# A three-stage decoder layer on one core: the start-up reordered, the mask analysed earlier, and the output transposes taken apart

## The reference, cut to what matters

```
x = x + self_attention(layernorm(x))       # 16 heads of 16; down (256 -> 16*64) and up (64 -> 16)
                                           # weights; half of each head is rotated (cos, sin)
x = x + cross_attention(layernorm(x), ctx, mask)      # mask (512, 512), True = key may be seen
x = x + mixture(layernorm(x))                         # router, top 512 tokens of 8 experts, two matmuls
```

## Time and profile before

| | |
|---|---|
| median of three runs | 1333.94 us (1333.66 to 1336.55) |
| the profiled execution: its own time | 1336.71 us |
| the profiled execution: first to last instruction | 1335.0 us |
| mean granted TensorE clock | 0.924 of full |
| first `st` matmul | 86.29 us |
| busy share PE / DVE / ACT / POOL | 86% / 76% / 51% / 39% |

### The profile page before, as it was taken

One profiled execution on the slowest core, in us unless ns is written; L12 is line 12 of the kernel. 1 busy time (PEld: TensorE's weight loads), 2 busy tenths in 40 slices (PEclk: granted clock), 3 DMA queues, 4 the chain that ended last, 5 costly groups with the idle time before them and its releaser, 6 DMA issues. The chain is left out here.

```text
span 1335.0 us, 22038 instructions
## 1 busy us (share of the span) xinstructions
PE 1144.6 (86%) x7591; PEld 681.5 (51%) x7592; DVE 1017.3 (76%) x2733; ACT 680.2 (51%) x1359; POOL 518.5 (39%) x712
## 2 busy tenths in 40 slices
PE   4389999999999999999999999999995115999994
PEld 2255546455455554445454454544343004988984
DVE  4778778888888778889888898988852884766651
ACT  4015455554545555666656566666661103556551
POOL 6365563754748332324232323231021003445432
PEclk9569899998999999999999999999997556999997
DMA  5431523515345253342525252423111502545422
GB/s 172 108 85 43 112 76 87 120 39 111 81 111 121 78 123 83 101 105 79 112 65 112 65 111 75 102 71 74 34 48 34 161 1 96 163 111 109 112 23 26
DMA packets 90416, 118.06 MB, mean 88 GB/s; under 512 B 13057, under 2 KB 60161, under 8 KB 90178
## 3 DMA queue, kind: packets, MB, share of 16 engines
q1 hardware_dynamic: 84162, 108.12, 31.6%
q0 software_dynamic: 6144, 8.52, 3.8%
HBM read 48.76 MB, written 16.91 MB: 49 GB/s over the span
## 5 line engine op out<-in xcount | busy, mean ns | idle before, releaser
L739 ACT ACTIVATE probs<-ps_st 128x512 f32<-128x512 f32 (+3 forms) x1024 | 477.5, 518 | 345.9 <-PE ps_st L583 340.9
L601 PE MATMUL ps_p<-kst,qst 63*128 63x512 f32 (+3 forms) x1024 | 381.9, 435 | 10.9 <-DVE mx L827 8.3
L583 PE MATMUL ps_st<-qst,kst 64*128 64x512 f32 (+3 forms) x1024 | 358.6, 419 | 16.3 <-ACT probs L739 14.7
L825 DVE TENSOR_REDUCE mx<-ps_p 128x1 f32<-128x512 f32 x512 | 323.1, 681 | 19.7 <-PE ps_p L601 18.6
L583 PEld LDWEIGHTS ps_st<-qst,kst 64*128 64x128 f32 x1024 | 165.7, 188 | 267.1 <-ACT probs L739 206.7
L827 DVE CUSTOM_DVE_ANT_0 ps_p<-ps_p,tri 128x128 f32<-128x128 f32 (+3 forms) x512 | 238.5, 514 | 18.6 <-PE ps_p L601 15.6
L564 PE MATMUL ps_o<-probs,vals 128*32 128x512 f32 (+3 forms) x2048 | 234.6, 531 | 13.8 <-POOL probs L475 13.8
L601 PEld LDWEIGHTS ps_p<-kst,qst 63*128 63x128 f32 x1024 | 170.6, 190 | 40.4 <-DVE mx L827 17.8
L422 POOL TENSOR_SCALAR lnw<-mv 128x4 f32<-128x4 f32 x24 | 5.6, 234 | 346.5 <-DVE mv L811 346.5
L475 POOL TENSOR_SCALAR_AFFINE_SELECT probs<-probs 128x512 f32<-128x512 f32 x128 | 79.1, 633 | 91.8 <-ACT probs L739 91.8
L1189 PE MATMUL moe_ps_y<-moe_w,moe_hid_h 128*128 128x256 f32 x512 | 94.7, 283 | 0.0
(11 more groups left out here) (203 smaller groups left out, 1879.5 us busy)
## 6 DMA issues: line engine op xcount, KB each, us to landing
qst<-qk_h SPq DMA_DIRECT2D x64, 256.0 KB, 4.8
kst<-qk_h SPq DMA_DIRECT2D x64, 256.0 KB, 5.0
qst<-qk_l SPq DMA_DIRECT2D x32, 256.0 KB, 5.5
kst<-qk_l SPq DMA_DIRECT2D x32, 256.0 KB, 5.2
moe_w1r<-in_w_dram SPq DMA_DIRECT2D x8, 1024.0 KB, 5.2
moe_w2r<-in_w_dram SPq DMA_DIRECT2D x8, 1024.0 KB, 8.9
xin<-in_x_dram SPq DMA_DIRECT2D x8, 512.0 KB, 4.0
xres<-in_x_dram SPq DMA_DIRECT2D x8, 512.0 KB, 3.9
```

Source lines behind the costliest of these rows:

```text
L583: last = nc.tensor.matmul(out, kst[rows, t % 2, pair, kt * P:(kt + 1) * P], qst[rows, t % 2, pair, lo:S], start=True, stop=not masked)
L601: last = nc.tensor.matmul(ps_p1[:, i % 3, 0:keys], qst[rows, t % 2, pair, qt * P:(qt + 1) * P], kst[rows, t % 2, pair, 0:keys], start=True ...
L739: nc.scalar.activation(probs[:, kt, j, 0:n], ps_st[:, i % 2, 0:n], ACT.Exp, scale=float(DH) ** -0.5).then_inc(exp_done, 1)
L825: nc.vector.tensor_reduce(mx[:, g % 2, at:at + 1], bank, AX.X, ALU.max).then_inc(max_done, 1)
```

## The change

Seven things are changed.

1. The mask is loaded ahead of the three `down` arrays, and VectorE analyses it right after `ln` 0. The counting matmuls go ahead of fold 0 and between turn 0 and fold 2. The 0/1 copy goes into a view of `xres` (`mask_ones`), so that the scaled copy can be made at once. Only the last piece (the key row) stays behind the four `qk` on TensorE and the rotations on VectorE.
2. ScalarE fills both `kst` (zeros) and `qst` (ones): buffer 0 at the start, by four activations, buffer 1 after the weights, by four more. GpSimd's memset of `qst` is gone. The row of ones is copied into `kst` for each buffer, just ahead of its first `stack`.
3. `xload` 1 is issued behind the rope table, ahead of `wc` and the small arrays; it waits for `xn` of batch 0.
4. `ln` 1 goes from behind the four `stack` and `qk` steps of turn 0 to in front of the first `qk`, for VectorE and GpSimd alike.
5. `xt` 1 and the first `qk` of turn 1 go together behind `v`, ahead of the first `p1`; the other three `qk` of turn 1 move 7 to 9 units ahead (old units of the four -29, -21, -13, -5, new -45, -28, -21, -14).
6. In every turn `ot` 0 goes from unit 19 to unit 3 of the turn after; it waits only for `og` of the second group.
7. The waits for the mask chain and for the row of ones move to where they are needed (`p1`, `st`).

```diff
     for t in range(TURNS):
         far, near, own, after = (SPAN * (t + i) for i in (-2, -1, 0, 1))
         put(far - SPAN + 14, "xload", t)
-        put(far + 10, "ln", t)
-        put(far + 23, "xt", t, 0)
-        put(far + 27, "xt", t, 1)
+        put(far + (-34 if t == 1 else 10), "ln", t)
+        put(far + (17 if t == 1 else 23), "xt", t, 0)
+        put(far + (18 if t == 1 else 27), "xt", t, 1)
         for i in range(4):
-            put(far + (35, 43, 51, 59)[i], "qk", t, i // 2, i % 2)
+            put(far + ((19, 36, 43, 50) if t == 1 else (35, 43, 51, 59))[i], "qk", t, i // 2, i % 2)
-        put(after + 19, "ot", t, 0)
+        put(after + 3, "ot", t, 0)
         put(after + 19, "ot", t, 1)
...
+            sp.dma_start(mask_u8, dram["mask_t"].rearrange("(a p) c -> p a c", p=P)).then_inc(mask_loaded, 16)
             for i in range(3):
                 sp.dma_start(down[i].rearrange("p (a c) -> p a c", a=8),
                              dram["down_t"][i].rearrange("(a p) c -> p a c", p=P)).then_inc(down_loaded[i], 16)
             sp.dma_start(late[:, :, :], dram["rope"].rearrange("a p s -> p a s")).then_inc(rope_loaded, 16)
-            sp.dma_start(mask_u8, dram["mask_t"].rearrange("(a p) c -> p a c", p=P)).then_inc(mask_loaded, 16)
+            xload(1)
...
-            nc.gpsimd.memset(qst[:, :, :, :].bitcast(F32), 1.0).then_inc(qst_ones, 1)
             nc.gpsimd.memset(vals[:, :, :, :].rearrange("p a b c -> p (a b c)"), 1.0).then_inc(pool_prep, 1)
+            run(STEPS[first:second])
             pool.wait_ge(rope_loaded, 16)
             pool.wait_ge(small_loaded, 80)
-            run(STEPS[first:])
+            run(STEPS[second:])
...
-                        pe.wait_ge(m_free, M[("og", GROUPS * t + 3)] + 1)
+                        pe.wait_ge(m_free, M[("og", GROUPS * t + 1 + 2 * k)] + 1)
...
+            pe.wait_ge(mask_chain, 1)
+            for kt in range(TT):
+                last = nc.tensor.matmul(ps_m[:, 0, :], ones, mask_ones[:, kt, :], start=(kt == 0), stop=(kt == TT - 1))
+            last.then_inc(mask_mm, 1)
             pe.wait_ge(up_loaded, 32)
             fold(0)
             fold(1)
             turn_weights(0)
+            pe.wait_ge(mask_chain, 5)
+            nc.tensor.matmul(ps_m[:, 1, 0:TT], ones, differs, start=True, stop=True).then_inc(mask_mm, 1)
             fold(2)
             turn_weights(1)
+            pe.wait_ge(mask_chain, 6)
             run(STEPS[:first], False)
             turn_weights(2)
             run(STEPS[first:second], False)
...
+            def clear(buf):
+                for rows, value, done in ((kst, zero, kst_zero), (qst, unit, qst_ones)):
+                    for half in range(2):
+                        nc.scalar.activation(rows[:, buf, 4 * half:4 * half + 4, :], value[:, :].unsqueeze(2).to_broadcast([P, 4, S]),
+                                             ACT.Copy).then_inc(done, 1)
-            act.wait_ge(zero_made, 1)
+            act.wait_ge(zero_made, 2)
             clear(0)
-            clear(1)
             raw(0)
-            clear(2)
             raw(1)
...
-            clear(3)
             act.wait_ge(wc_loaded, 16)
             nc.scalar.activation(wo[:, 0, :, :], wc_raw.rearrange("p (a c) -> p a c", a=KT), ACT.Copy).then_inc(prep_hi, 1)
+            clear(1)
```

More of the change, by code:

```diff
@@ L321, in _ @@
                 kind = s[0]
-                if kind == "xload" and s[1] > 0:
+                if kind == "xload" and s[1] > 1:
                     xload(s[1])
@@ L405, in _ @@
             nc.gpsimd.memset(zero[:, :], 0.0).then_inc(zero_made, 1)
+            nc.gpsimd.memset(unit[:, :], 1.0).then_inc(zero_made, 1)
             nc.gpsimd.memset(up[:, :, :], 0.0).then_inc(up_zero, 1)
@@ L684, in _ @@
             run(STEPS[first:second], False)
-            pe.wait_ge(mask_chain, 1)
+            pe.wait_ge(mask_chain, 8)
             for kt in range(TT):
[L687 to L691, removed]
-            for kt in range(TT):
-                last = nc.tensor.matmul(ps_st[:, 1, kt * P:(kt + 1) * P], key_cols[:, kt, :], identb[:, :], start=True, stop=True)
+                last = nc.tensor.matmul(ps_p1[:, 0, kt * P:(kt + 1) * P], key_cols[:, kt, :], identb[:, :], start=True, stop=True)
             last.then_inc(mask_mm, 1)
@@ L924, in _ @@
             second = STEPS.index(("xt", 0, 1)) + 1
-            third = STEPS.index(("ln", 1)) + 1
+            third = STEPS.index(("qk", 0, 1, 1)) + 1
             nc.vector.memset(ones, 1.0)
             run(STEPS[:first])
+            dve.wait_ge(mask_loaded, 16)
+            mask_link(nc.vector.tensor_scalar(out=mask_ones, in0=mask_u8, scalar1=1.0, scalar2=None, op0=ALU.mult))
+            mask_link(nc.vector.tensor_scalar(out=lower_t[:, :, :], in0=mask_u8, scalar1=BIG, scalar2=-BIG, op0=ALU.mult, op1=ALU.add))
+            dve.wait_ge(mask_mm, 1)
+            mask_link(nc.vector.tensor_scalar(out=some_key[:, :], in0=ps_m[:, 0, :], scalar1=1.0, scalar2=None, op0=ALU.min), False)
+            nc.vector.tensor_reduce(keepers, lower_t[:, :, :], AX.X, ALU.max)
+            mask_link(nc.vector.tensor_reduce(keep_all, lower_t[:, :, :], AX.X, ALU.min))
+            mask_link(nc.vector.tensor_tensor(out=differs, in0=keepers, in1=keep_all, op=ALU.subtract), False)
+            dve.wait_ge(mask_mm, 2)
+            mask_link(nc.vector.tensor_reduce(vary_sum, ps_m[:, 1, 0:TT], AX.X, ALU.add))
+            nc.vector.tensor_scalar(out=vary[0:1, 0:1], in0=vary_sum[0:1, 0:1], scalar1=0.0, scalar2=None, op0=ALU.is_gt)
+            mask_link(nc.vector.tensor_scalar(out=alike, in0=vary_sum, scalar1=0.0, scalar2=None, op0=ALU.is_equal))
+            mask_link(nc.vector.tensor_tensor(out=key_cols, in0=keepers.unsqueeze(2).to_broadcast([P, TT, P]),
+                                              in1=alike.unsqueeze(2).to_broadcast([P, TT, P]), op=ALU.mult), False)
             low_qk(0)
@@ L934, in _ @@
             run(STEPS[second:third])
-            dve.wait_ge(mask_loaded, 16)
-            mask_link(nc.vector.tensor_scalar(out=lower_t[:, :, :], in0=mask_u8, scalar1=1.0, scalar2=None, op0=ALU.mult))
             dve.wait_ge(prep_hi, 4)
```

36 lines of the change are left out of this document (13 added, 23 removed).

## The result

The changed kernel takes **1316.37 us** (median of 4 runs, 1314.4 to 1317.02) against 1333.8 for the kernel before in the same comparison (4 runs, 1332.57 to 1336.55): a ratio of 0.9862, 95% interval 0.9848 to 0.9876. It is 1.4% or 17.4 us faster. The profiled execution took 1315.83 us with a span of 1314.1. The span before was 1335.0, so between the profiled executions there are 20.9 us; of the 3.5 us by which this is more than the 17.4, 2.9 are the distance of the profiled execution of before from its median and 0.5 that of after.

A forecast was written before the change was run, and what follows sets the result against it. A chain across engines was taken to bound the start-up, and TensorE, nearly always busy, the turns. Start-up -5.5, `ot` 0 -1.7 and last turn -0.7 made -7.9 us: 1333.94 becomes 1326 us, range 1318 to 1332.

The forecast's parts named there:

- the term for `ot` 0: Seven self-attention turns: moving `ot` 0 saves 0.25 us each, -1.7 us in all, bounds -4 and +2.
- rival 1: Self-attention turns: TensorE's clock may not fall where `ot` 0 goes, at most -10 us; under 1322 us, chance 0.17.
- my signs of being wrong: Whole kernel: turns after the first grow, or the first `st` comes later than 84 or earlier than 77 us.
- Rival 3: First units of a turn: `ot` 0 delays the scores serially, about +15 us over fifteen turns, 1342 us; chance 0.04.
- Cross-attention: Cross-attention turns: TensorE is packed in both places of `ot` 0, so 0 us, bounds -2 and +2.
- The tail: Last turn: `y` waits for the chain of one half less, -0.7 us.
- The start-up: Up to the first `st`: it comes at 80.8 instead of 86.29 us, -5.5 us, bounds -3 and -9.
- `ln` 1 on GpSimd: Start-up, ahead of GpSimd's first rotation: normalizing batch 1 takes between 5.3 and 7.5 us, half way taken.
- From there to the first `st`: Start-up, behind the last `qk` of turn 1: `shift` sets 7.1 us instead of 1.92, giving back 5.2.
- Rival 2: Start-up: slower rotations and late stacks eat the gain, leaving 0 to -2 us, 1332 to 1334; chance 0.12.
- 5.7 us lost and 15.3 won around `ln` 1: Start-up: third rotation 5.7 us later; last rotation to first `qk` of turn 1 takes 9.3 us instead of 24.6.
- the stacks of turn 0: Start-up: they land by 53 to 54 us, about when the `qk` is through, losing at most 1 us.

The follow-up runs named there:

- experiment 1: Kernel before with only `ot` 0 moved, from unit 19 to unit 3, and its wait: 1321.37 us, ratio 0.9898.
- Experiment 2: Changed kernel with `ot` 0 put back to unit 19: 1331.01 us, ratio 0.9971.
- experiment 3: Kernel before with four useless transposes of `ident` added at unit 3 of turns 1 to 7: 1327.92 us, ratio 0.9949.
- experiment 4: Kernel before with eight useless transposes of `ident` added at unit 3 of turns 1 to 7: 1327.7 us, ratio 0.9954.
- Experiment 5: Kernel before with `ot` 0 at unit 10 instead of 19: 1343.57 us, ratio 1.0077.
- experiment 6: Kernel before with only the mask load and analysis moved early: 1328.77 us, ratio 0.9957.
- experiment 7: Changed kernel with `ln` 1, `xt` 1 and the four `qk` of turn 1 at their old units: 1315.09 us, ratio 0.9861.
- Kernel 10: Changed kernel with GpSimd's half of `ln` 1 behind both its turn 0 rotations, `xt` and `qk` of turn 1 at old units: 1311.3 us, again 1315.95.

## Why the prediction was wrong

**The step that failed is the term for `ot` 0.** I put -0.25 us a turn and -1.7 in all, with bounds of -4 and +2. Turns 1 to 7 gave 12.2 us, and experiment 1 alone 13.2. Two things were wrong in it. The direct part was halved: I let the copy of ScalarE weigh against the shorter stretch, but the first group did not grow (5.54 against 5.56), so the 0.6 us of the third group came nearly whole: -3.9 instead of -1.7. And the clock was left out of the term and given to rival 1 with a chance of 0.17, though its price was worked out from the right rows: "five turns of 2.0 give -10 at the utmost", and 1326 less 10 is the time that was measured, in part by luck: the clock gave about 8 us, and most of the rest is the direct part. What I held against the rival was that an earlier start-up redraws the stretches. Experiment 2 shows that their sum stays: 328.68 us in six turns after a shift of 6 us. My own row said where to look: the stretch lay across the first sixteen units of a turn, whose first eight are the lightest in the turn, TensorE busy 4.25 of 5.56 us. The Trainium skill, "TensorE: Matmul & The Clock Gate", section "What's actually happening", has activity lift the clock; experiments 3 and 4 agree with it (1327.92 and 1327.7 us with work added), and I had cited it beside the rival without letting it move the chance. None of my signs of being wrong showed this: the turns did not grow, and the first `st` lay between 77 and 84; none of them asked whether the stretches would go.

**Rival 3, `ot` 0 on the scores' path,** did not come at unit 3: the first group takes what it took. Experiment 5 shows that the danger was real seven units later, where the room is gone: +1.28 us in that group at clock 1.00, and slower in all.

**Cross-attention:** forecast 0, measured -1.1 us in seven turns, inside the bounds of -2 and +2, and `ot` 0's own: experiment 1 takes 427.2 us for them, experiment 2 428.2, as before. **The tail:** I had -0.7; the `y` of the last turn still waits 1.53 us for `ot_l` (before 1.69), and the rest of the program is 0.7 us longer. The term is 0.

**The start-up** was right as a mechanism and near in size. Between the two profiled executions the first `st` moved by -8.1 us (86.29 to 78.22), against -5.5 forecast and inside the bounds of -3 and -9. But the same start-up as before also runs in experiments 1, 3, 4 and 5, with the first `st` at 84.65, 85.32, 84.12 and 85.13, and that of the changed kernel in experiment 2 and in its repetition, at 79.8 and 78.66. The means are 85.1 of five and 78.9 of three: -6.2 us, and the 8.1 compares the latest of the one with the earliest of the other. Step by step, in the two profiled executions:

- Loads, forecast +0.7: the fold that started at 14.09 starts at 14.47, so +0.4, and the first `qk` of turn 0 is no later than before (22.34 against 22.84).
- The mask, forecast 0: right, and `ln` 0 beside it took GpSimd 6.5 us (8.27 to 14.8), hidden as worked out.
- `ln` 1 on GpSimd, forecast half way between 5.3 and 7.5 us: it took 6.7 (24.66 to 31.38). Longer instructions beside VectorE's rotation are in the row (2.77 us for the four, against 2.18 in the earlier trace rows, while VectorE ran its rotation until 29.91, three instructions of which have two inputs in SBUF), as the Trainium skill, "SBUF — State Buffer", section "Who interferes with whom", has it. The third rotation came at 36.16, forecast 37.8 (whose lower bound, 31.2 and 5.5, is 36.7 and not 36.5; nothing hangs on it).
- The first `qk` of turn 1 at VectorE: 52.07, forecast 54.5. The first `p1` near 54: 54.18.
- The spacing of the four: 19.65 us in all, forecast 19.2. The last at 71.72, forecast 73.7.
- From there to the first `st`: 6.5 us, forecast 7.1. TensorE did not wait for `shift`, as I had said that it would: `shift` was issued at 75.15, the second transfer 0.7 later, and the `st` that needs it runs 3.07 us after the first issue. So it landed in less than 2.4 us; I had 3.3, by a neighbour of another size. The view of TensorE's waits from 28 to 79 us has no `shift` in it:

```profile
PE ps_m L545 <- DVE rope L872: 8.4, 1, 8.4
PE ps_p L609 <- DVE mx L836: 6.9, 5, 4.2
PE ps_m L623 <- DVE vals L893: 2.9, 1, 2.9
PE ps_p L609 <- DMA kst<-qk_h: 2.2, 1, 2.2
PE ps_m L545 <- DVE xt_l L847: 1.6, 1, 1.6
```

Its columns are the wait, its time in all, how often and the longest.

Rival 2, the gain eaten in the rotations, did not come either, though `ln` 1 took nearly its price: the first `st` is 6 to 8 us earlier, not 0 to 2.

But I read the gain wrongly in one respect, which the sum hid: it needs none of the new units. The early mask gives all of it (experiment 6), and the step that I priced most closely, 5.7 us lost and 15.3 won around `ln` 1, is the mask alone: 12.5 of the 15.3 are its old place, and the new units, with the 5.7 that they cost, net to nothing (experiment 7). What is late next is not in my list of waits with its right weight: the stacks of turn 0. From 37.50 to the first `p1` all 16 DMA engines are busy throughout (share 1.03):

```profile
37.50:54.18 16.68, 10.04 (x38) 8.38 (x39) 11.29 (x19) 1.19 (x2) 5.21 (x4) 0.65 1.03 217
```

I had "about when the `qk` is through; at most 1 us is lost"; TensorE lost 2.15 there, and GpSimd, whose rotation may write its buffer only when these copies have read it, 0.8. Kernel 10, whose stacks go out at 39.2, has its first `p1` at 49.30 and its first `st` 3.4 us earlier.

**What stays open.** Which turn gets a stretch in an execution: the changed kernel had its one in turn 6 in one profile, and in turns 4 and 7 in another. Whether four transposes are enough in most executions, since the profile of experiment 3 is of its slowest run. And turn 7: some 2.5 of the clock's 8 us are its two short stretches, far behind the first units. The changed kernel had none of them, experiment 1 one, experiment 3 none and experiment 4 both, so it is not shown that work in the first units takes these away.

## What to carry to other kernels

In a loop where TensorE is over 90% busy, look for the lightest stretch of an iteration and read the granted clock right behind it: moving work into it can pay twice, once where it leaves and once by the clock, and where it goes decides the sign (-13 us at one place, +9 us seven units later). Before a shorter chain is credited to the many moves of a change, try each move alone: here one of the start-up's moves gave all that could be measured. Where a rival's price comes from good rows, the argument against it needs rows as well.

## What the runs showed of the hardware

- Adding transposes that nobody reads, about 0.5 us of TensorE work a turn in seven turns, made the kernel 6.6 us faster (1327.92 against 1334.57), the doubled amount 7.2 us (1327.7 against 1334.9).
- A stretch of 6.8 us at half clock cost 2.0 to 2.2 us where TensorE had some slack around it (turns of 55.64 to 55.79 against 53.62), and 2.5 us in a packed group (10.40 against 7.92).
- Of 18 self-attention turns whose first eight units have TensorE busy some 4.25 of 5.56 us, 13 held a stretch at half clock; of 48 with four transposes more in those units, 6 did. TensorE was busy 93% and 94% of such a turn at clock 1.00.
- The same start-up in five executions (before and experiments 1, 3, 4 and 5) had its first `st` between 84.12 and 86.29: one profile of each kernel does not settle a difference of 2 us.
